# Moving elementwise tiles between the slots of a software-pipelined attention loop on Trainium2

## The reference, cut to what matters

```python
# 8 images, each 256 rows of 256 pixels with 3 channels, and 128 text tokens of 256 values
g = einsum('bhwc,cd->bhwd', x, ccm) + ccm_bias              # base colours: 3x3 mixing
g = sum(slopes * relu(g[..., None] - shifts), axis=-1)      # curve (one live point here)
h = clip(einsum('bhwc,co->bhwo', g, conv_w) + conv_b, 0, 1) # an image row = a token of 256
h = concatenate([h, txt], axis=1)                           # 384 tokens per batch
h = h + attention(layernorm(h))      # 16 heads of 16, causal, latent keys and values, W_O
h = h + moe(layernorm(h)) + bias     # 8 experts, top 2, capacity tokens/8, gelu, 256-1024-256
```

## Time and profile before

| what | value |
|---|---|
| median of 3 runs | 676.55 us (675.48 to 676.63) |
| the profiled execution | 675.31 us, span 673.6 us |
| PE busy | 619.4 us, 92% |
| DVE busy | 394.4 us, 59% |
| ACT busy | 377.4 us, 56% |
| POOL busy | 396.6 us, 59% |
| granted TensorE clock | 0.983 of full, 1.00 in each stretch from 68 to 298 us |

### The profile page before, as it was taken

The page is one execution under the profiler, slowest core; times in us unless marked ns, Lnnn a source line. Parts: engine busy times, 40 slices in busy tenths (PEclk is TensorE's granted clock), DMA queues, the critical chain, the costliest instruction groups (busy, mean ns, idle before and its releaser), DMA issues.

```text
span 673.6 us, 13929 instructions
## 1 busy us (share of the span) xinstructions
PE 619.4 (92%) x5184; PEld 516.3 (77%) x5184; DVE 394.4 (59%) x940; ACT 377.4 (56%) x818; POOL 396.6 (59%) x605
## 2 busy tenths in 40 slices
PE   2698999999999899999888899999999999999992
PEld 2465566666657566666578899999999999999992
DVE  4788787778988888678644243344444444444320
ACT  4357776767677675666541354544454554554540
POOL 3313233424646446455765589988888888888223
PEclk9999999999999999999996999999999999999997
DMA  6527574633524233361111633544444444442123
GB/s 224 159 67 205 171 215 138 190 93 88 158 79 121 60 83 100 96 226 44 50 63 64 194 139 61 152 86 104 92 96 99 108 110 106 106 110 43 22 24 39
DMA packets 66604, 73.86 MB, mean 110 GB/s; under 512 B 6312, under 2 KB 61586, under 8 KB 66536
## 3 DMA queue, kind: packets, MB, share of 16 engines
q1 hardware_dynamic: 56232, 59.45, 29.2%
q0 software_dynamic: 9504, 13.00, 11.0%
q10 hardware_dynamic: 800, 0.52, 0.3%
HBM read 31.62 MB, written 22.48 MB: 80 GB/s over the span
## 4 chain that ended last, share of the span: by engine, by line
PE 73%; DVE 8%; ACT 6%; issue 5%; DMA 3%; POOL 3%; ACTq 0%; DVEq 0%; SPq 0%; POOLq 0%
PE t_bank L1686 20%; PE bank L1701 14%; PE s_bank L1701 7%; PE bank L672 5%; PE t_bank L637 4%; PE s_bank L615 3%; PE t_bank L730 3%; DVE mx L1125 3%; PE t_bank L785 2%; PE s_bank L616 2%; PE s_bank L1671 1%; PE bank L684 1%; POOL slot_rows L528 1%; PE t_bank L715 1%; PE bank L762 1%
## 5 line engine op out<-in xcount | busy, mean ns | idle before, releaser
L1648 DVE TENSOR_TENSOR hl<-h,hh 128x384 fp32r<-128x384 f32 x128 | 103.4, 814 | 156.4 <-ACT h L1611 156.4
L540 POOL TENSOR_SCALAR_AFFINE_SELECT pt<-pt 128x256 f32<-128x256 f32 x192 | 86.2, 456 | 153.0 <-ACT pt L930 117.4
L1125 DVE TENSOR_REDUCE mx<-s_bank 128x2 f32<-128x256 f32 (+2 forms) x192 | 122.3, 682 | 46.2 <-PE s_bank L616 46.0
L1608 ACT ACTIVATE hh<-t_bank 128x384 fp32r<-128x384 f32 x128 | 63.0, 492 | 134.0 <-PE t_bank L1686 131.8
L1561 POOL DMA_INDIRECT out<-yo,xr x48 | 74.8, 1559 | 59.1 <-ACT yo L1619 49.1
L930 ACT ACTIVATE pt<-t_bank 128x512 f32<-128x512 f32 x128 | 76.1, 601 | 39.6 <-PE t_bank L637 38.4
L1548 POOL TENSOR_TENSOR wl<-wr,wh 128x256 fp32r<-128x256 f32 x112 | 95.1, 883 | 1.2
L1686 PE MATMUL t_bank<-xh,wh 128*128 128x384 f32 x256 | 86.3, 337 | 0.9 <-DVE xl L1642 0.9
L1686 PE MATMUL t_bank<-xl,wh 128*128 128x384 f32 x256 | 85.9, 335 | 0.0
L1686 PE MATMUL t_bank<-xh,wl 128*128 128x384 f32 x256 | 85.8, 335 | 0.0
L615 PE MATMUL s_bank<-ks,qs 96*128 96x128 bf16 (+2 forms) x384 | 79.1, 275 | 2.9 <-DMA ks<-part 2.5
(11 more groups left out here) (188 smaller groups left out, 1349.4 us busy)
## 6 DMA issues: line engine op xcount, KB each, us to landing
wr<-in_w SPq DMA_DIRECT2D x16, 1024.0 KB, 5.9
qs<-part SPq DMA_DIRECT2D x96, 96.0 KB, 2.2
ks<-part SPq DMA_DIRECT2D x90, 96.0 KB, 2.2
slot_rows<-empty SPq DMA_DIRECT2D x4, 1560.0 KB, 8.8
xr<-slot_rows SPq DMA_DIRECT2D x16, 390.0 KB, 3.3
wr<-in_x SPq DMA_DIRECT2D x8, 768.0 KB, 5.5
out<-hid SPq DMA_DIRECT2D x8, 384.0 KB
qs<-mT ACTq DMA_DIRECT2D x64, 3.0 KB
```

What stands on the lines that cost most here:

```text
L540: pool.affine_select(out=blocks, in_=blocks, compare_op=ALU.is_ge, fill=0.0, base=0, pattern=[[0, 2], [1, P]], channel_multiplier=-1).then ...
L1125: ins = dve.tensor_reduce(mx[:, p // 2, j, 2 * (p % 2):2 * (p % 2) + 2], pair_region(s_bank, j), AX_X, ALU.max)
L1648: dve.tensor_tensor(hl[:, f, :], h[f % 2][:, :], hh[:, f, :].bitcast(F32), ALU.subtract).then_inc(hl_done, 1)
```

## The change

ScalarE: base colours d = 1 of odd turns go from step 1 to step 0, before `exps(n, 0, 2)`, and d = 2 in step 1 from behind `exps(n, 1, 2)` to behind `exps(n, 1, 0)` (both to that place in turn -1). The copy of the second transposed token part goes from before `exps(n, 1, 0)` to before `contexts` of step 0. The relu of channel 0 goes from the end of step 0 of even turns to before `exps(n, 0, 2)`, and in turn 0 to step 1. VectorE: `curve` of the first channel, and `norms2` of tile 2 with `variances2` (odd turns before 16), go to step 1 between the two groups of maxima; turn 0 keeps its curve in one piece, and turn 17 its statistics. No instruction is added or removed, and TensorE's, POOL's and SP's lists are the same.

```diff
--- before.py
+++ after.py
@@ -1027,11 +1027,12 @@
             for p in range(4):
                 if p == 3 and prev:
                     contexts_out(n - 1, 0)
-                if odd and p == 1 and late(b + 2):
-                    tokens_back(b + 2, 1, 1)
                 if cur:
                     exps(n, p, 0)
 
+                if odd and p == 1 and live(b + 3):
+                    for d in (1, 2) if n == FIRST else (2,):
+                        colours(b + 3, d)
                 if odd and p == 1 and late(b + 2):
                     latents(b + 2, 1)
                 if ahead(n, p, 0):
@@ -1048,6 +1049,8 @@
                 if n == 0 and p in (1, 2):
                     for k in (2, 3):
                         query_key(1, k, 2 * p - 2)
+                if n == 0 and p == 1:
+                    relus(b + 2, 0)
                 if not odd and p == 1 and live(b + 2):
                     relus(b + 2, 1)
                 if cur:
@@ -1057,8 +1060,12 @@
                 if p == 2 and nxt:
                     max_rows(n + 1, 0)
 
+                if not odd and p == 0 and live(b + 2) and n:
+                    relus(b + 2, 0)
                 if odd and p == 0 and late(b + 2):
                     tokens_back(b + 2, 0, 1)
+                if odd and p == 0 and live(b + 3) and n != FIRST:
+                    colours(b + 3, 1)
                 if ahead(n, p, 1):
                     query_key(*ahead(n, p, 1))
                 if odd and p == 3 and live(b - 1) and b - 1 < B - 1:
@@ -1070,8 +1077,6 @@
                         query_key(1, k, 1)
                 if odd and p == 3 and b - 1 == B - 1:
                     rows_back(b - 1, 0)
-                if odd and p == 1 and live(b + 3):
-                    colours(b + 3, 1)
                 if not odd and p == 1 and live(b + 2):
                     relus(b + 2, 2)
                 if not odd and p == (3 if n < OVER else 2) and live(b - 2):
@@ -1079,6 +1084,8 @@
                 if cur:
                     exps(n, p, 2)
 
+                if odd and p == 0 and late(b + 2):
+                    tokens_back(b + 2, 1, 1)
                 if p == 0 and prev:
                     contexts(n - 1, 1)
                 if p == 2 and cur:
@@ -1086,8 +1093,6 @@
                 if n == 0 and p == 0:
                     for k in (0, 1):
                         query_key(1, k, 2)
-                if not odd and p == 0 and live(b + 2):
-                    relus(b + 2, 0)
                 if n == FIRST and p == 0:
                     for i in range(2):
                         token_values(0, i, i)
@@ -1102,8 +1107,6 @@
                 if live(b + 3):
                     if (p == 0 and n == FIRST) or (p == 3 and not odd):
                         colours(b + 3, 0)
-                    if p == 1 and odd:
-                        colours(b + 3, 2)
                 if odd and p == 3 and b - 1 == B - 1:
                     rows_back(b - 1, 1)
                 if n == OVER and p == 3:
@@ -1352,6 +1355,12 @@
             for p in range(4):
                 if nxt:
                     maxima(n + 1, p, 0)
+                if not odd and p == 1 and live(b + 2) and n:
+                    curve(b + 2, (0,))
+                if odd and p == 1 and live(b - 1) and n < OVER:
+                    norms2(b - 1, (2,))
+                    variances2(b - 1)
+                if nxt:
                     maxima(n + 1, p, 1)
                 if n == FIRST and p == 0:
                     scaled(1)
@@ -1379,8 +1388,8 @@
                             colours(b + 3, i)
                     if p == 0 and live(b - 1) and n < OVER:
                         residual(b - 1, 1)
-                    if p == 1 and live(b - 1):
-                        norms2(b - 1, (2,) if n < OVER else range(NT))
+                    if p == 1 and n == OVER + 1:
+                        norms2(b - 1, range(NT))
                         variances2(b - 1)
                     if p == 1 and routed:
                         weigh(b - 2)
@@ -1404,7 +1413,7 @@
                         if n >= OVER:
                             choose(b - 2)
                     if p == 1 and live(b + 2):
-                        curve(b + 2)
+                        curve(b + 2, (1, 2) if n else range(CH))
                     if p == 2 and live(b + 2):
                         curve_rest(b + 2)
                         norms(b + 2)
```

## The result

The changed kernel takes **668.66 us** (median of 4 runs, 667.52 to 669.37) against 676.59 for the kernel before, run beside it (675.48 to 678.77). The ratio is 0.9871, with a 95% interval of 0.9846 to 0.9896: 0.0129 x 676.6 = 8.7 us less (interval 7.0 to 10.4); the two medians differ by 7.9. The profiled execution took 667.52 with a span of 665.8 (before: 675.31 and 673.6).

What follows compares the result with a forecast made beforehand. TensorE, holding 73% of the chain of waits, bounds the kernel, so only its idle time counts. Terms -5.4 -1.9 -1.8 -0.6 +0.1 +0.6 +0.4 = -8.6 gave 668.0; own range 666 to 670, wider 665.6 to 672.4.

Steps and rivals of the forecast that it cites:

- Part 1: Base colours out of step 1 in odd turns: TensorE's gap at L735 closes, 1.08 in five turns, 5.4 off.
- Part 2: Second token copy before contexts: starts 0.38 earlier, shortening L715's wait in turns 3 to 11, 1.9 off.
- Part 3: Curve's first channel between two groups of maxima: L708's wait for VectorE shrinks in turns 5 to 11, 1.8 off.
- the late case: Moved curve instruction waits until POOL's adds end, maxima are 0.11 late, and the term is 0.53 instead of 0.64.
- Part 4: Relu of channel 0 moved: 0.6 off in turn 2, 0.6 on in turn 0, nothing in later even turns.
- Turn 1: Shorter first hole on ScalarE: tile d = 1 may delay exps and second token copy, 0.1 on, bounds 0 to 0.81.
- Turn -1: Tile d = 2 only changes places with two token copies, all before the copy of the maxima: 0.
- Part 5: Statistics between the groups of maxima: free in turns 3 to 11, 0.4 on in turn 13, 0 in turn 15.
- A: Rival: only the L735 gap closes, the other two are swallowed; about 5 off, 671.5; chance 0.15.
- B: Rival: the stall at L735 returns a few instructions later and the turn stays 40 us; 676; chance 0.05.
- C: Rival: ScalarE has no hole for the two moved colour tiles, so odd turns lose; 679; chance 0.05.
- D: Rival: turns gain the same, but the attention part's end, POOL's row scatters between selects, keeps half; 672; chance 0.05.

Runs made afterwards that it cites:

- e1: The changed kernel with base colours d = 1 and 2 back in their old places; 672.98 us, ratio 0.9932.
- e4: The changed kernel with the second token copy again behind contexts and before exps(n,1,0); 670.45 us, ratio 0.9895.
- e3: The changed kernel with curve in one piece again, behind the maxima of step 1; 670.81 us, ratio 0.9893.
- e6: The changed kernel with the relu of channel 0 behind contexts again in even turns above 0; 670.75 us, ratio 0.9895.
- e10: The changed kernel with only turn 0's relu back in its old place; 669.38 us, ratio 0.9858.
- e5: The changed kernel with turns -1, 0 and 13 in the old order and turn 1's two colour tiles both in step 1; 666.16 us, ratio 0.9858.
- e11: The changed kernel with turns -1, 0 and 13 in old order and turn 1's colour tiles in step 1, run again; 667.45 us, ratio 0.9844.
- e9: The changed kernel once more, without any edit; 670.98 us, ratio 0.9878 against the kernel before.
- e7: The changed kernel with norms2 of tile 2 and variances2 again behind both groups of maxima; 670.22 us, ratio 0.9893.
- e2: The kernel before with only the two base colour tiles moved; 673.09 us, ratio 0.9929.
- e8: The changed kernel with each moved colour tile of turns 1 to 9 computed twice, once into a spare tile; 673.42 us, ratio 0.9949.
- e12: The changed kernel with POOL's three residual adds one step later, away from the moved curve instruction; 669.75 us, ratio 0.9880.

## Why the prediction was right

Forecast 668.0, measured 668.66; in the span 665.0 against 665.8. Step by step:

- **Part 1 (5.4).** Right. 1.08 in every turn from 3 to 9, in the change and in e1. Turn 11 of the kernel before, which has no colours, had given the number.
- **Part 2 (1.9).** Right: 5 x 0.39 = 1.93 (e4). The limit was the 0.38 by which the copy moved. It gives 0.38 in turn 1, too, but of a wait that only the d = 1 tile makes there.
- **Part 3 (1.8).** Right in kind, a little small: 2.0 in the table (0.35, 0.63, 0.50, 0.51), 2.1 in e3. The step took the gap of turn 9 for those of 7 and 11; its own rule, bracket plus 0.16, gives 0.33, 0.65, 0.51 and 0.51 for the brackets of before, 0.17, 0.49, 0.35 and 0.35, together 2.0, as measured. Its bound for the late case, 0.53, assumed that the moved instruction waits until all three adds end. It waited 0.24 (0.32 in turn 4), the maxima behind were not late, and turn 7 gave 0.63. So its time went over 0.7, which the prediction had named as one half of a sign of being wrong; the other half, late maxima, stayed away.
- **Part 4 (0.6 off, 0.6 on).** Right: -0.58 in turn 2 (e6), +0.55 to +0.6 in turn 0 (e10, e5), nothing in the later even turns.
- **Turn 1 (0.1 on) failed in size.** It gave back 0.7 of its 1.08. Of this some 0.4 is the pair of DMA issues, which took 1.61 in turn 1 here against 1.20 before and is no work that anybody moved; 0.3 is the d = 1 tile, which delays the second token copy, as its sentence had feared. The copy's transposes do end as the tile ends (68.11 + 0.52 = 68.63, 67.86 + 0.80 = 68.66), as the step said; but exps(1, 0, 2) stands between tile and copy and starts only at 68.57. The prediction also had not listed the 0.43 that L708 of this turn waits in the kernel before, at 66.79, for the copy behind the pair of issues: a turn with that wait has no slack for a slower pair. In e5, with no tile in step 0 of this turn and a pair of 1.41, 0.5 of the 0.7 is back. ScalarE, turn 1:

```profile
65.81 1.61 ACTq L942 DMA_DIRECT2D qs<-mT  x2
67.48 0.49 ACT L977 ACTIVATE xnT<-t_bank 128x384 f32<-128x384 f32 x1 [1.22 <-issue]
67.86 0.80 ACT L964 ACTIVATE g<-wr,prm 128x512 f32<-128x512 f32 x1
69.05 0.49 ACT L977 ACTIVATE xnT<-t_bank 128x384 f32<-128x384 f32 x1
```

- **Turn -1 (0) failed by 0.2 to 0.3.** The step looked for a reader of the late token copies and found none that minds; it forgot that the copy also sets a bank free, which the transposes of the maxima (L645) want:

```profile
40.04 0.33 PE L645 MATMUL bank<-ident_b,ms 128*8 128x128 bf16 x3 [0.34 <-ACT xnT L977]
```

In e11 the copies are early again, L645 waits 0.15, for VectorE, and latents begins 0.2 sooner after the scores. The other 0.1 was there before L645, at 36 us. e9, with the new order and the clock at half for longer, waits 0.15 for VectorE, too: there the scores are late enough to hide the copies.
- **Part 5 (0.4 on) failed in size.** Turn 13 lost 0.1, and of that -0.06 (e7), +0.1 (e5) and -0.1 (e11) came off on undoing it, no more than e9 differs. The second group of maxima is late, much as the step said: it starts at 295.35 with no idle time in front, 0.3 later than before against the marks (303.31 - 8.28 = 295.03). But the instruction behind it that makes the low parts takes 0.15 instead of 0.36:

```profile
304.25 0.36 DVE L1138 TENSOR_TENSOR ms<-mx,ms 128x12 bf16<-128x12 f32 x1
```

```profile
296.26 0.15 DVE L1141 TENSOR_TENSOR ms<-mx,ms 128x12 bf16<-128x12 f32 x1
```

In the kernel before it ended with POOL's three selects (303.45 + 1.15 = 304.60), and so it does in e2, e5, e7 and e11, which have the statistics in their old place (0.36 or 0.37; in e7 297.35 + 0.37 against 296.54 + 1.15). With the new place it starts only as the selects end, and takes 0.15 in each of the nine profiles. That it waited for POOL is read from these ends and was not tested apart. So 0.2 of the 0.3 was time that VectorE would have waited anyway: the step charged the work and not the wait behind it. L645 of turn 13 now follows a wait for a DMA:

```profile
296.17 0.39 PE L637 MATMUL t_bank<-qs,ks 98*128 98x384 bf16 x2 [0.29 <-DMA qs<-mT]
296.49 0.33 PE L645 MATMUL bank<-ident_b,ms 128*8 128x128 bf16 x3
```

This wait is not the statistics' doing: e7, without them, has 0.22 there, e8 0.80 and e12 none, in which L645 waits 0.16 for VectorE.
- **The end** gives 0.4 back. No experiment took it apart, but the two traces say where. Behind the last values the clock stretches differ (half from 333.3 to 336.7 and from 350.3 to 357.2 us after, from 356.6 to 366.8 before), and they cancel: at POOL's last scatter of rows the changed kernel is 8.1 ahead (375.24 - 367.12). At the first matmul of the experts it is 7.7 ahead (377.73 - 370.02). Before, TensorE came to it from its transposes L785 without idle time; after, it waits for the DMA that reads the rows back:

```profile
370.02 0.88 PE L1680 MATMUL s_bank<-ident,xr 128*128 128x128 f32 x6 [0.47 <-DMA xr<-slot_rows]
```

The misses (turn -1 +0.3, turn 1 +0.6, turn 13 -0.3, part 3 -0.2, the end +0.4) add to 0.8, which is what the span shows. They have both signs, so that the total is as close as 0.8 is in part luck; the sizes of parts 1 to 4, 9.7 of work taken out against 9.9 measured, are not.

Of the rivals, A is out (e3 and e4: the two other gaps are worth 2.1 and 1.9), B is out (no bracket behind L735 in turns 3 to 11, and the marks keep what was won), C is out at one tile per hole in turns 3 to 9 and begins with the second (e8), in turn 1 it holds for 0.3, and D holds for 0.4 at most and not for half, and that behind the last scatter, not between the selects. The order of reading had most to do with it: TensorE's brackets first, then what the releaser did before each.

On the Trainium skill's rule ("SBUF — State Buffer", section "Who interferes with whom"), that VectorE's two-port mode and GpSimd exclude each other: the trace shows both sides paying, the moved instruction 0.78 instead of 0.54, the three adds 2.28 instead of 2.11, and e12 and e3 show that each is the other's doing. (In which mode the instruction runs no row shows.) That is 0.24 for one instruction against 2.28 of adds that lie around it, so the wait was for at most one add (2.28 / 3 = 0.76, an estimate), not for the run of them. Charged with one add, the maxima would have come out as not late, as they were.

## What to carry to other kernels

On an engine that bounds the kernel, list its few idle brackets per loop turn, and look for a turn of the same trace in which the suspected instruction is absent: the difference between such a turn and its neighbours gave 1.08 to the hundredth. A moved tile is free while its hole is longer than the tile, but it uses up the slack that covered other things, here a pair of DMA issues that takes 1.2 us in most turns and up to 1.9 in turns 1 and 3. Work put in front of another instruction costs only what the wait behind it does not swallow (part 5). The first and last turns of a pipeline have other holes than the middle: cost each from its own rows (readers, and banks that a copy sets free), and give it an order of its own, which was worth about 1.5 us here by the marks of e11.

## What the hardware did that I had not expected

**The clock in turn 0.** In seven of the nine profiled executions with turn 0's relu in its new place (e1, e3, e4, e6 to e9) TensorE's granted clock fell to the lower level, 1.2 GHz, at values of turn 0, between 0.7 us before their start and 0.2 behind it, and the 24 matmuls took 2.61 to 2.79 instead of 1.50; the marks behind it are 1.3 to 1.5 later. In all five with the relu in its old place (before, e2, e5, e10, e11) it stayed at 2.4 GHz. TensorE's idle times just before are 0.76 and 0.89 with the new place, 0.65 and 0.89 with the old one. What the two orders differ in is 0.1 us of idle time, so the link is suggested by 12 of 14 profiles and not shown.

There is a rival in the same profiles. Before turn 0 the clock was at half once already, until 35.8 to 36.9 us in seven of them (before, the changed kernel, e2, e7, e10 to e12) and until 37.8 to 38.9 in the other seven (e1, e3 to e6, e8, e9), in kernels with either order. Of the seven with the later end six fell again in turn 0, of the seven with the earlier end only e7. The two explanations part in four profiles: e5 (old place, later end, no fall) and the changed kernel and e12 (new place, earlier end, no fall), and e7 (new place, earlier end, fall); each explanation has its misses, and nothing here varies one alone.

The Trainium skill ("TensorE: Matmul & The Clock Gate", section "Part 1: The HAM clock gate") says that half rate is the default and activity releases it; the trace agrees in so far as the clock fell behind idle time and came back under matmuls (in e9 at 59.4 and 62.8 us). If the link with the relu holds, the new place of this one relu costs 0.6 always and 1.3 more most times. The medians of e9 and e10 (670.98, 669.38) point this way, their intervals (0.9855 to 0.9900, 0.9836 to 0.9881) don't separate them.

**The clock near the end.** Another dip comes in five of the profiles at values of turn 15 (the changed kernel, e2, e6, e7, e9). The chain of the changed kernel's profile shows it:

```profile
332.79 2.38 PE bank L672 x24
```

One kernel's runs spread with the mean granted clock: e10 took 665.31 at 0.985 and 669.45 at 0.978 of the full clock in the mean. That spread of 4 us is as large as parts 2 and 3 together; only the marks resolve single parts. The dip of turn 15 lies behind the mark of the changed kernel, so it is in no row of the table.

**ScalarE's DMA issues.** The pair at L942 holds ScalarE's queue for 1.19 to 1.27 us in most turns. In turn 1 it took 1.20 and 1.26 in before and e2, 1.35 to 1.88 in the other profiles; in turn 3 1.22 to 1.95. What lengthens it stays open. The DMA engines were busier in the early turns (a share of 0.88 from 65 to 68 us in the changed kernel, 0.08 from 180 to 185), but the kernel before had 0.92 from 65 to 68 with its pair of 1.20, and nothing here varies that alone.
